# Head attention of a four-layer graph network: eight batches written out, the weighted sums carried over the batch boundary

## The chip, the cores and the metric

The kernel runs on one core of one Trainium2 chip, in one launch. The metric is the device time in microseconds; three runs of a kernel give its median. A profile is one further execution, with its own time beside its span.

## The reference, cut to what matters

Four graph layers act on x of shape (8, 2048, 128) with one 2048 x 2048 adjacency. Layers 0 and 3 are graph attention with one head, layer 2 is a mean over neighbours. The change touches layer 1 alone, attention with 4 heads of 32 features over all nodes:

```
q = (x @ W_q).reshape(Bn, Nn, NUM_HEADS, HEAD_DIM).transpose(0, 2, 1, 3)
k = (x @ W_k)...    # the same shape
v = (x @ W_v)...    # the same shape
scores = jnp.einsum('bhnd,bhmd->bhnm', q, k) / np.sqrt(HEAD_DIM).astype(np.float32)
scores = jnp.where(adj == 0, -jnp.inf, scores)
attn = jax.nn.softmax(scores, axis=-1)
out = jnp.einsum('bhnm,bhmd->bhnd', attn, v)
```

## The kernel before

The kernel is a row of stages, each with a program of its own for TensorE (pe), VectorE (dve), ScalarE (act), GpSimd (pool) and SyncE (sp), tied by semaphores. `head_attention` is the longest. For each batch it takes the four heads as two pairs (u = 0, 1), each pair's 2048 query rows as four chunks of 512, and each chunk against the 2048 keys as T = 16 tiles of 128. So a batch is eight chunks of 16 steps, BODY = 128 steps, and the stage is 8 x 128 = 1024 steps. A step g does this:

- pe: a *slot* (L1175 to L1191), two small matmuls of q and k into `mx_ps`, from which the row maximum of the chunk two further on is found; then the two *scores* matmuls of the step, one for each head, into `sc_ps` (L1231); then `weigh` (L1193 to L1207), the weighted sum of the step LAG = 3 earlier, `w` times `v` into `o_ps`, in float32.
- act: two exponentials from `sc_ps` to `w` (L1314); at the step LAG after a chunk's end, `keep_rows` copies the chunk's sums from `o_ps` to `oe` (L1303).
- pool masks `w` in three steps of four (L1327), dve in the fourth (L1276). dve also takes the maxima of the slot (two reductions, L1263), and once in a chunk joins them (L1270) and writes the row shift `mshift` (L1252).
- sp, once in a chunk, stores the chunk before (`store`: four DMAs) and sends the shift through memory into the extra row of `qs` (`place_shift`: one DMA, a wait for it, two DMAs). At chunk 4 it loads q and k of the next batch for pair 0 (`load`: twelve DMAs) and `v`; at the batch's end the same for pair 1. Each load waits until the scores (or sums) that read the old contents are done.

`w` has PB = 4 buffers, `sc_ps` and `mx_ps` two each, `o_ps` and `oe` two, by the chunk's parity.

All engines run the batches as a hardware loop (`Fori(0, B)`, L1150, L1216, L1287, L1308, L1321) whose body is the 128 steps written out. The counts that they wait for depend on the loop's variable, so they are worked out in registers before the wait. In the loop, pe does `weigh` for steps 0 to 124 in steps 3 to 127 and then the last three in a row (L1238, L1239), and only then branches back; act keeps the last chunk's rows there (L1317). In the last batch the slots of chunks 6 and 7 find maxima for two chunks that do not exist, and sp loads batch 0 once more (`following`).

Of the kernel before, what the change touches and what calls it, by code (L numbers as in the profile page):

```python
# [18 lines left out]
B = 8  # L19
N = 2048  # L20
F = 128
T = N // P
# [3 lines left out]
CH = N // BANK  # L26
# [1012 lines left out]
def head_attention(nc, io, keep):  # L1039
# [11 lines left out]
    BODY = 2 * STEPS  # L1051
    CHUNKS = 2 * CH
    RT = T // CH
    UNITS = RT * CH
    TURN = UNITS // 4
# [4 lines left out]
    with ExitStack() as stack:  # L1060
# [47 lines left out]
        def of_step(jt):  # L1108

            return [k for k, n in enumerate(slots(False)) if (TURN if n < 0 else n) == jt]  # L1110

        def ring(k, chunk_parity):

            return (k + chunk_parity) % MB
# [13 lines left out]
        @block.sync  # L1128
        def _(sp):
            load(sp, 0, 0)  # L1130
            for t in range(T):
                sp.dma_start(mbias[:, t, :], io["mask_bias"][t * P:(t + 1) * P, :]).then_inc(
                    mbias_early if t < 2 * RT else mbias_loaded, 16)
            load_v(sp, 0, 0)
            load(sp, 0, 1)
            load_v(sp, 0, 1)
            place_shift(sp, 0, 0, 0)

            def store(b, c):

                sp.wait_ge(o_kept, 2 * CH * b + c + 1 + 2)
                u, rows = c // CH, slice(c % CH * BANK, (c % CH + 1) * BANK)
                for a in range(2):
                    head = 2 * u + a
                    sp.dma_start(io["heads_t"][bass.ds(b, 1), head * HD:(head + 1) * HD, rows].rearrange("one p n -> p (one n)"),
                                 oe[2 * HD * a:2 * HD * a + HD, c % 2, :]).then_inc(o_stored[c % 2], 16)
                    sp.dma_start(io["sums"][bass.ds(b, 1), head:head + 1, rows].rearrange("one p n -> p (one n)"),
                                 oe[2 * HD * a + HD:2 * HD * a + HD + 1, c % 2, :]).then_inc(o_stored[c % 2], 16)

            with sp.Fori(0, B) as b:  # L1150
                following = (b + 1) % B
                for c in range(CHUNKS):
                    if c == CH:
                        sp.wait_ge(scored, 2 * (BODY * b + STEPS))
                        load(sp, following, 0)
                    if c >= 1:
                        store(b, c - 1)
                    place_shift(sp, CHUNKS * b + c + 1, (c + 1) % CHUNKS // CH, (c + 1) % CH)
                    if c == CH:
                        sp.wait_ge(weighed, BODY * b + STEPS + PB)  # L1160
                        load_v(sp, following, 0)
                sp.wait_ge(scored, 2 * BODY * (b + 1))
                load(sp, following, 1)
                store(b, CHUNKS - 1)
                sp.wait_ge(weighed, BODY * (b + 1) + PB)
                load_v(sp, following, 1)
            for u in range(2):
                sp.wait_ge(qk_loaded[u], LOADS * (B + 1))
                sp.wait_ge(v_loaded[u], 16 * (B + 1))
                sp.wait_ge(o_stored[u], 64 * CH * B)  # L1170
            sp.wait_ge(shift_placed, 32 * (CHUNKS * B + 1))

        @block.tensor
        def _(pe):
            def slot(k, chunk, u, c, first=False):  # L1175

                n, buf = slots(first)[k], ring(k, c % 2)
                if n < 0 and first:
                    return
                if n < 0:  # L1180
                    pe.wait_ge(rows_done, chunk)
                pe.wait_ge(mx_taken, SLOTS * chunk + k + 1)
                if n < 0:
                    mm = nc.tensor.transpose(mx_ps[0:2 * RT, buf, 0, 0:P], mrow[:], keep["ident"][:])
                else:
                    t, kc = RT * c + n // CH, n % CH
                    for a in range(2):
                        hi = slice(a * HD, (a + 1) * HD)
                        mm = nc.tensor.matmul(mx_ps[:, buf, a, :], qs[u][a][hi, t * P:(t + 1) * P], ks[u][a][hi, kc * BANK:(kc + 1) * BANK],  # L1189
                                              start=True, stop=True)  # L1190
                mm.then_inc(mx_scored, 1)  # L1191

            def weigh(g, i):  # L1193

                u, c, jt = g // STEPS, g // T, g % T
                if jt == 0:
                    pe.wait_ge(o_kept, 2 * CH * i + c + 1)
                if g % STEPS == 0:
                    pe.wait_ge(v_loaded[u], 16 * (i + 1))
                if g in mine:  # L1200
                    pe.wait_ge(masked_dve, len(mine) * i + mine.index(g) + 1)
                else:
                    pe.wait_ge(masked_pool, (BODY - len(mine)) * i + g - sum(m < g for m in mine) + 1)
                for a in range(2):
                    mm = nc.tensor.matmul(o_ps[2 * HD * a:2 * HD * a + HD + 1, c % 2, :], v[u][:, jt, a, :], w[:, g % PB, a, :],  # L1205
                                          start=(jt == 0), stop=(jt == T - 1))
                mm.then_inc(weighed, 1)  # L1207

            pe.sem_inc(weighed, PB)
            pe.sem_inc(mx_scored, 1)  # L1210
            pe.wait_ge(qk_loaded[0], LOADS)
            for chunk in range(2):
                for k in range(SLOTS):
                    slot(k, chunk, 0, chunk, chunk == 0)
            pe.wait_ge(units_ready, 4)
            with pe.Fori(0, B) as i:  # L1216
                for g in range(BODY):
                    u, r = g // STEPS, g % STEPS
                    c, jt = r // T, r % T
                    on, tu, tc = target(g // T)  # L1220
                    if jt == 0 and tc == 0:
                        pe.wait_ge(qk_loaded[tu], LOADS * (i + on + 1))
                    mine_now = of_step(jt)
                    slot(mine_now[0], CHUNKS * i + g // T + 2, tu, tc)
                    if jt == 0:
                        pe.wait_ge(shift_placed, 32 * (CHUNKS * i + g // T + 1))
                    for a in range(2):
                        n = 2 * g + a

                        pe.wait_ge(exp_done, 2 * BODY * i + (n + 1 if n else SB))  # L1230
                        nc.tensor.matmul(sc_ps[:, n % SB, :], ks[u][a][:, jt * P:(jt + 1) * P],  # L1231
                                         qs[u][a][:, c * BANK:(c + 1) * BANK], start=True, stop=True).then_inc(scored, 1)

                    if g >= LAG:
                        weigh(g - LAG, i)
                    for k in mine_now[1:]:
                        slot(k, CHUNKS * i + g // T + 2, tu, tc)
                for g in range(BODY - LAG, BODY):  # L1238
                    weigh(g, i)  # L1239

        @block.vector
        def _(dve):
            def slot(k, chunk, c, parity, masks, first=False):

                n, buf = slots(first)[k], ring(k, c % 2)
                if n < 0 and first:
                    return
                due = SLOTS * chunk + k + 1
                if n < 0:
# [4 lines left out]
                    dve.wait_ge(shift_ready, chunk)  # L1254
                    dve.sem_inc(mx_taken, 1)
                else:
                    if not isinstance(due, int):
                        dve.compute_val(due)
                    dve.wait_ge(*masks)
                    dve.wait_ge(mx_scored, due)  # L1260
                    t, kc = RT * c + n // CH, n % CH
# [22 lines left out]
            for chunk in range(2):  # L1284
                for k in range(SLOTS):
                    slot(k, chunk, chunk, chunk, (mbias_early, 16 * 2 * RT), chunk == 0)
            with dve.Fori(0, B) as i:  # L1287
                for g in range(BODY):
                    if g >= 1:
                        mask(g - 1, i)  # L1290
                    for k in of_step(g % T):
                        slot(k, CHUNKS * i + g // T + 2, target(g // T)[2], g // T % 2, (mbias_loaded, 16 * (T - 2 * RT)))
                mask(BODY - 1, i)

        @block.scalar
        def _(act):
# [8 lines left out]

            act.sem_inc(exp_done, SB)
            act.sem_inc(o_kept, 2)
            with act.Fori(0, B) as i:  # L1308
                for g in range(BODY):
                    act.wait_ge(weighed, BODY * i + g + 1)  # L1310
                    for a in range(2):
                        n = 2 * g + a
                        act.wait_ge(scored, 2 * BODY * i + n + 1)
                        nc.scalar.activation(w[:, g % PB, a], sc_ps[:, n % SB], ACT.Exp, scale=SCALE).then_inc(exp_done, 1)  # L1314
                    if g >= T + LAG and (g - LAG) % T == 0:
                        keep_rows((g - LAG) // T - 1, i)
                keep_rows(2 * CH - 1, i)  # L1317

        @block.gpsimd
        def _(pool):  # L1320
            with pool.Fori(0, B) as i:  # L1321
                for g in range(BODY):
                    if g in mine:
                        continue
# [533 lines left out]
```

## Time and profile before

| | |
|---|---|
| median of 3 runs | 3907.07 us (3902.50 to 3911.31) |
| the profiled execution, its own time | 3912.55 us |
| its span, first to last instruction | 3910.80 us |
| busy in the span | PE 3535.3 us (90%), DVE 3162.2 (81%), POOL 1820.8 (47%), ACT 1732.2 (44%) |
| mean granted TensorE clock | 0.939 |
| exponentials of the head attention, first start | 931.3 us |
| its last sums start | 2877.00 us |

The span is 1.75 us shorter than the execution's own time. The stage of the change takes half of the span, from about 930 to about 2880 us. PE, DVE, ACT and POOL are the busy times of matmul, VectorE, ScalarE and GpSimd; PEld is the weight load beside the matmuls; SPq, PEldq are the instructions on an engine's queue that are not counted as busy. In timelines, the bracket is the idle time ahead of a row and what ended it; "issue" means that the profile shows nothing that the engine waited for. Rows that follow each other on an engine are merged in timelines.

### The profile page before, as it was taken

To read this page: it belongs to the slowest core of one execution; us is meant where nothing else is said; L and a number is where in the kernel's file an instruction comes from. 1 tells how busy PE (TensorE), PEld (TensorE's weight loads), DVE (VectorE), ACT (ScalarE), POOL (GpSimd) and SP (SyncE) were. 2 spreads that over 40 slices of the span, in tenths; PEclk is the share of its full clock that TensorE was granted. 3 is DMA by queue.
4 is the path that set the end of the run, shared out by engine and by line. 5 is a ranking of instruction groups with operands and counts; after the bars stand their busy time and mean duration, and the time that the engine had idled before them with its cause. 6 is when DMAs were issued, how large, how long until landed. Compare 5 with 4: busy or idle time off the path is not lost. (4 is left out here: it accounts for less than half of the span.)

```text
span 3910.8 us, 71249 instructions
## 1 busy us (share of the span) xinstructions
PE 3535.3 (90%) x21228; PEld 1849.5 (47%) x21228; DVE 3162.2 (81%) x7145; ACT 1732.2 (44%) x3560; POOL 1820.8 (47%) x854
## 2 busy tenths in 40 slices
PE   5669999666999999999999999999968799789999
PEld 4669999441111111111111111111116599689999
DVE  6768888658999989999898998989967555367777
ACT  7811111552656656566565665656625423311100
POOL 2300000113888878888888887888843101100000
PEclk8779999886999999999999999999977799899999
DMA  6422121462100110001101010100125534221211
GB/s 238 168 100 82 50 87 50 154 232 104 27 19 14 29 27 27 21 12 29 27 27 26 8 27 27 27 23 11 28 90 210 199 144 155 101 91 68 82 65 45
DMA packets 66868, 288.66 MB, mean 74 GB/s; under 512 B 12483, under 2 KB 14917, under 8 KB 47045
## 3 DMA queue, kind: packets, MB, share of 16 engines
q1 hardware_dynamic: 64228, 267.55, 19.5%
q0 software_dynamic: 2304, 16.84, 1.0%
q8 instruction: 185, 3.03, 0.3%
q14 instruction: 151, 1.23, 0.1%
HBM read 174.12 MB, written 110.23 MB: 73 GB/s over the span
## 5 line engine op out<-in xcount | busy, mean ns | idle before, releaser
L1327 POOL TENSOR_TENSOR a_w<-a_w,keep_mask_t 128x1024 f32<-128x1024 f32 x768 | 1635.7, 2155 | 407.2 <-ACT a_w L1314 407.1
L1263 DVE CUSTOM_DVE_ANT_0 a_mx_ps<-a_mx_ps,a_mbias 128x512 f32<-128x512 f32 x2112 | 1389.4, 719 | 142.1 <-PE a_mx_ps L1189 129.6
L1314 ACT ACTIVATE a_w<-a_sc_ps 128x512 f32<-128x512 f32 x2048 | 1111.4, 595 | 812.3 <-PE a_sc_ps L1231 810.9
L1205 PE MATMUL a_o_ps<-a_w,a_v 128*33 128x512 f32 x4096 | 1083.6, 609 | 5.7 <-POOL a_w L1327 5.7
L839 PE MATMUL g_acc<-g_hv,g_w 128*128 128x129 f32 x8192 | 924.5, 276 | 36.4 <-ACT g_hv L797 24.8
L839 PEld LDWEIGHTS g_acc<-g_hv,g_w 128*128 128x128 f32 x8192 | 923.1, 193 | 38.1 <-DVE g_w L776 38.1
L776 DVE SCALAR_TENSOR_TENSOR g_w<-g_row,keep_s,keep_mask_t 128x1024 f32<-128x1024 f32 x512 | 647.2, 1282 | 203.7 <-PE g_acc L839 184.4
L1231 PE MATMUL a_sc_ps<-a_qs,a_ks 97*128 97x512 f16 x2048 | 634.4, 392 | 0.0
L1189 PEld LDWEIGHTS a_mx_ps<-a_ks,a_qs 32*128 32x128 f16 x2112 | 94.8, 91 | 893.9 <-DVE a_mx L1263 469.3
L1189 PE MATMUL a_mx_ps<-a_ks,a_qs 32*128 32x512 f16 x2112 | 411.3, 396 | 77.5 <-DVE a_mx L1263 33.4
L1276 DVE TENSOR_TENSOR a_w<-a_w,keep_mask_t 128x1024 f32<-128x1024 f32 x256 | 460.2, 1798 | 0.7
L1205 PEld LDWEIGHTS a_o_ps<-a_w,a_v 128*33 128x33 f32 x4096 | 151.4, 109 | 449.0 <-issue 287.6
L1263 DVE DVE_READ_ACCUMULATOR2_ANT a_mx<- 128x1 f32 x2112 | 288.8, 137 | 0.0
L1231 PEld LDWEIGHTS a_sc_ps<-a_qs,a_ks 97*128 97x128 f16 x2048 | 125.9, 97 | 241.6 <-issue 201.8
L1757 PE MATMUL p_sum_ps<-p_g,keep_mask_t 128*128 (+1 forms) x2048 | 232.4, 275 | 3.0 <-DMA p_g<-g 3.0
L919 POOL MEMSET p_minus_half<- 128x16 f32 x1 | 0.1, 116 | 493.5 <-POOLq L664 493.5
L1757 PEld LDWEIGHTS p_sum_ps<-p_g,keep_mask_t 128*128 128x128 bf16 x2048 | 201.8, 99 | 27.3 <-DMA p_g<-g 3.1
L101 POOL TENSOR_TENSOR p_rstd<-p_tmp,p_minus_half 128x16 f32<-128x16 f32 x24 | 69.8, 2910 | 290.7 <-DVE p_tmp L88 290.7
L794 ACT COPY g_value<-keep_s 128x16 f32 (+1 forms) x16 | 3.3, 204 | 437.6 <-DMA g_h<-h_nodes 425.8
L803 ACT ACTIVATE g_e<-g_y 128x1024 f32<-128x1024 f32 x16 | 16.9, 1058 | 328.8 <-DVE g_y L741 328.8
L1672 DVE SCALAR_TENSOR_TENSOR p_part<-p_sum_ps,keep_rdeg,p_own 128x128 f32<-128x128 f32 x128 | 44.6, 349 | 121.0 <-PE p_sum_ps L1757 119.9
L1735 ACT ACTIVATE p_hn<-p_x,p_shift,p_rstd 128x128 f32<-128x128 f32 x128 | 50.1, 479 | 115.9 <-DVE p_shift L94 115.9
(178 smaller groups left out, 2278.2 us busy)
## 6 DMA issues: line engine op xcount, KB each, us to landing
p_x<-x SPq DMA_DIRECT2D x24, 1024.0 KB, 8.3
g_h<-h_nodes SPq DMA_DIRECT2D x16, 1032.0 KB, 6.2
p_adj_in<-in_adj SPq DMA_DIRECT2D x16, 1024.0 KB, 7.8
g_row<-u_rows SPq DMA_DIRECT2D x32, 512.0 KB, 7.3
a_v<-v SPq DMA_DIRECT2D x18, 528.0 KB, 3.6
a_ks<-k_hi SPq DMA_DIRECT2D x72, 128.0 KB, 2.8
a_qs<-q_hi SPq DMA_DIRECT2D x72, 128.0 KB, 3.0
v<-p_v SPq DMA_DIRECT2D x8, 1056.0 KB, 6.8
```

Source lines behind the costliest of these rows:

```text
L101: nc.gpsimd.tensor_tensor(rstd, tmp[:, 3, :], minus_half, ALU.pow).then_inc(rooted, 1)
L776: nc.vector.scalar_tensor_tensor(out=w[:, g % PB, :], in0=row[:, k, cols], scalar=keep["s2_08"][:, bass.ds(b, 1), jt], in1=keep["mask_t"][ ...
L839: mm = nc.tensor.matmul(tile(half, it), w[:, g % PB, it * P:(it + 1) * P], hv[:, k, jt, :], start=(jt == 0 and it % 3 == 0), stop=(jt == T ...
L1189: mm = nc.tensor.matmul(mx_ps[:, buf, a, :], qs[u][a][hi, t * P:(t + 1) * P], ks[u][a][hi, kc * BANK:(kc + 1) * BANK], start=True, stop=True)
L1205: mm = nc.tensor.matmul(o_ps[2 * HD * a:2 * HD * a + HD + 1, c % 2, :], v[u][:, jt, a, :], w[:, g % PB, a, :], start=(jt == 0), stop=(jt = ...
L1231: nc.tensor.matmul(sc_ps[:, n % SB, :], ks[u][a][:, jt * P:(jt + 1) * P], qs[u][a][:, c * BANK:(c + 1) * BANK], start=True, stop=True).the ...
L1263: last = nc.vector.tensor_tensor_reduce(out=mx_ps[:, buf, a, :], in0=mx_ps[:, buf, a, :], in1=mbias[:, t, kc * BANK:(kc + 1) * BANK], scal ...
L1276: nc.vector.tensor_tensor(w[:, g % PB], w[:, g % PB], keep["mask_t"][:, jt, c * BANK:(c + 1) * BANK].unsqueeze(1).to_broadcast([P, 2, BANK ...
L1314: nc.scalar.activation(w[:, g % PB, a], sc_ps[:, n % SB], ACT.Exp, scale=SCALE).then_inc(exp_done, 1)
L1327: nc.gpsimd.tensor_tensor(w[:, g % PB], w[:, g % PB], keep["mask_t"][:, jt, c * BANK:(c + 1) * BANK].unsqueeze(1).to_broadcast([P, 2, BANK ...
L1735: last = nc.scalar.activation(hn[:, t, :], x3[:, t, :], ACT.Relu, bias=shift[:, t:t + 1], scale=rstd[:, t:t + 1])
L1757: mm = nc.tensor.matmul(sum_ps[:, it % SLOTS, 0:2 * F], keep["mask_t"][:, jt, it * P:(it + 1) * P], of(g, b)[:, 0, jt, :], start=(jt == 0) ...
```

## The change

All five loops over the batches become Python loops, so that 8 x 128 steps are written out and every count is a constant. pe does the sums of steps 125 to 127 of a batch in steps 0 to 2 of the next batch; act keeps the last chunk's rows after step 3 of the next batch; sp stores them at the next batch's first chunk and loads pair 1's `v` behind that store, ahead of the shift of chunk 1. In the last batch sp loads nothing, the shift for the chunk that does not exist is not placed, and `wanted` leaves out the slots from chunk 64 on, other than the first four of chunk 64 and the transpose of the real last chunk's maxima.

```diff
--- before.py
+++ after.py
@@ -1109,6 +1109,12 @@
 
             return [k for k, n in enumerate(slots(False)) if (TURN if n < 0 else n) == jt]
 
+        def wanted(n, chunk):
+
+
+
+            return chunk < CHUNKS * B or chunk == CHUNKS * B and n in (-1, *range(TURN))
+
         def ring(k, chunk_parity):
 
             return (k + chunk_parity) % MB
@@ -1147,35 +1153,36 @@
                     sp.dma_start(io["sums"][bass.ds(b, 1), head:head + 1, rows].rearrange("one p n -> p (one n)"),
                                  oe[2 * HD * a + HD:2 * HD * a + HD + 1, c % 2, :]).then_inc(o_stored[c % 2], 16)
 
-            with sp.Fori(0, B) as b:
-                following = (b + 1) % B
+            for b in range(B):
+                more = b < B - 1
                 for c in range(CHUNKS):
-                    if c == CH:
+                    if c == CH and more:
                         sp.wait_ge(scored, 2 * (BODY * b + STEPS))
-                        load(sp, following, 0)
+                        load(sp, b + 1, 0)
                     if c >= 1:
                         store(b, c - 1)
-                    place_shift(sp, CHUNKS * b + c + 1, (c + 1) % CHUNKS // CH, (c + 1) % CH)
-                    if c == CH:
+                    elif b > 0:
+                        store(b - 1, CHUNKS - 1)
+                        sp.wait_ge(weighed, BODY * b + PB)
+                        load_v(sp, b, 1)
+                    if more or c < CHUNKS - 1:
+                        place_shift(sp, CHUNKS * b + c + 1, (c + 1) % CHUNKS // CH, (c + 1) % CH)
+                    if c == CH and more:
                         sp.wait_ge(weighed, BODY * b + STEPS + PB)
-                        load_v(sp, following, 0)
-                sp.wait_ge(scored, 2 * BODY * (b + 1))
-                load(sp, following, 1)
-                store(b, CHUNKS - 1)
-                sp.wait_ge(weighed, BODY * (b + 1) + PB)
-                load_v(sp, following, 1)
+                        load_v(sp, b + 1, 0)
+                if more:
+                    sp.wait_ge(scored, 2 * BODY * (b + 1))
+                    load(sp, b + 1, 1)
+            store(B - 1, CHUNKS - 1)
             for u in range(2):
-                sp.wait_ge(qk_loaded[u], LOADS * (B + 1))
-                sp.wait_ge(v_loaded[u], 16 * (B + 1))
                 sp.wait_ge(o_stored[u], 64 * CH * B)
-            sp.wait_ge(shift_placed, 32 * (CHUNKS * B + 1))
 
         @block.tensor
         def _(pe):
             def slot(k, chunk, u, c, first=False):
 
                 n, buf = slots(first)[k], ring(k, c % 2)
-                if n < 0 and first:
+                if n < 0 and first or not wanted(n, chunk):
                     return
                 if n < 0:
                     pe.wait_ge(rows_done, chunk)
@@ -1213,15 +1220,16 @@
                 for k in range(SLOTS):
                     slot(k, chunk, 0, chunk, chunk == 0)
             pe.wait_ge(units_ready, 4)
-            with pe.Fori(0, B) as i:
+            for i in range(B):
                 for g in range(BODY):
                     u, r = g // STEPS, g % STEPS
                     c, jt = r // T, r % T
                     on, tu, tc = target(g // T)
-                    if jt == 0 and tc == 0:
+                    chunk = CHUNKS * i + g // T + 2
+                    if jt == 0 and tc == 0 and chunk < CHUNKS * B:
                         pe.wait_ge(qk_loaded[tu], LOADS * (i + on + 1))
                     mine_now = of_step(jt)
-                    slot(mine_now[0], CHUNKS * i + g // T + 2, tu, tc)
+                    slot(mine_now[0], chunk, tu, tc)
                     if jt == 0:
                         pe.wait_ge(shift_placed, 32 * (CHUNKS * i + g // T + 1))
                     for a in range(2):
@@ -1233,17 +1241,19 @@
 
                     if g >= LAG:
                         weigh(g - LAG, i)
+                    elif i > 0:
+                        weigh(BODY + g - LAG, i - 1)
                     for k in mine_now[1:]:
-                        slot(k, CHUNKS * i + g // T + 2, tu, tc)
-                for g in range(BODY - LAG, BODY):
-                    weigh(g, i)
+                        slot(k, chunk, tu, tc)
+            for g in range(BODY - LAG, BODY):
+                weigh(g, B - 1)
 
         @block.vector
         def _(dve):
             def slot(k, chunk, c, parity, masks, first=False):
 
                 n, buf = slots(first)[k], ring(k, c % 2)
-                if n < 0 and first:
+                if n < 0 and first or not wanted(n, chunk):
                     return
                 due = SLOTS * chunk + k + 1
                 if n < 0:
@@ -1254,8 +1264,6 @@
                     dve.wait_ge(shift_ready, chunk)
                     dve.sem_inc(mx_taken, 1)
                 else:
-                    if not isinstance(due, int):
-                        dve.compute_val(due)
                     dve.wait_ge(*masks)
                     dve.wait_ge(mx_scored, due)
                     t, kc = RT * c + n // CH, n % CH
@@ -1284,7 +1292,7 @@
             for chunk in range(2):
                 for k in range(SLOTS):
                     slot(k, chunk, chunk, chunk, (mbias_early, 16 * 2 * RT), chunk == 0)
-            with dve.Fori(0, B) as i:
+            for i in range(B):
                 for g in range(BODY):
                     if g >= 1:
                         mask(g - 1, i)
@@ -1305,7 +1313,7 @@
 
             act.sem_inc(exp_done, SB)
             act.sem_inc(o_kept, 2)
-            with act.Fori(0, B) as i:
+            for i in range(B):
                 for g in range(BODY):
                     act.wait_ge(weighed, BODY * i + g + 1)
                     for a in range(2):
@@ -1314,11 +1322,13 @@
                         nc.scalar.activation(w[:, g % PB, a], sc_ps[:, n % SB], ACT.Exp, scale=SCALE).then_inc(exp_done, 1)
                     if g >= T + LAG and (g - LAG) % T == 0:
                         keep_rows((g - LAG) // T - 1, i)
-                keep_rows(2 * CH - 1, i)
+                    if g == LAG and i > 0:
+                        keep_rows(2 * CH - 1, i - 1)
+            keep_rows(2 * CH - 1, B - 1)
 
         @block.gpsimd
         def _(pool):
-            with pool.Fori(0, B) as i:
+            for i in range(B):
                 for g in range(BODY):
                     if g in mine:
                         continue
```

## Rows read from the trace of the kernel before

**Rows 1.** Page: busy line of PE, and the granted clock in 40 slices, tenths.
```profile
PE 3535.3 (90%) x21228; PEld 1849.5 (47%) x21228; DVE 3162.2 (81%) x7145; ACT 1732.2 (44%) x3560; POOL 1820.8 (47%) x854
PEclk8779999886999999999999999999977799899999
```

**Rows 2.** Windows inside a batch: busy PE, PEld, DVE, ACT, POOL, clock, DMA share, GB/s.
```profile
2675.00:2822.30 147.30, 147.30 (x647) 28.46 (x645) 141.18 (x351) 91.98 (x171) 127.63 (x61) 1.00 0.08 20
```

**Rows 3.** ScalarE's timeline: `keep_rows`, inside a batch and at batch ends.
```profile
1170.88 1.17 ACT L1303 COPY a_oe<-a_o_ps 33x512 f32<-33x512 f32 x2 [3.61 <-PE a_o_ps L1205]
...
1456.13 1.16 ACT L1303 COPY a_oe<-a_o_ps 33x512 f32<-33x512 f32 x2
...
1632.91 1.16 ACT L1303 COPY a_oe<-a_o_ps 33x512 f32<-33x512 f32 x2
...
1901.78 1.17 ACT L1303 COPY a_oe<-a_o_ps 33x512 f32<-33x512 f32 x2 [3.61 <-PE a_o_ps L1205]
...
2144.58 1.17 ACT L1303 COPY a_oe<-a_o_ps 33x512 f32<-33x512 f32 x2 [3.61 <-PE a_o_ps L1205]
...
2878.10 1.17 ACT L1303 COPY a_oe<-a_o_ps 33x512 f32<-33x512 f32 x2 [3.61 <-PE a_o_ps L1205]
```

**Rows 4.** TensorE's timeline inside a batch: start, length, operation.
```profile
1308.84 0.39 PE L1189 MATMUL a_mx_ps<-a_ks,a_qs 32*128 32x512 f16 x2
1309.16 0.60 PE L1231 MATMUL a_sc_ps<-a_qs,a_ks 97*128 97x512 f16 x2
1309.70 1.05 PE L1205 MATMUL a_o_ps<-a_w,a_v 128*33 128x512 f32 x4
1310.68 0.39 PE L1189 MATMUL a_mx_ps<-a_ks,a_qs 32*128 32x512 f16 x2
```

**Rows 5.** TensorE's timeline over the second batch boundary.
```profile
1409.14 2.77 PE L1205 MATMUL a_o_ps<-a_w,a_v 128*33 128x512 f32 x12
1412.62 1.05 PE L1205 MATMUL a_o_ps<-a_w,a_v 128*33 128x512 f32 x4 [0.71 <-POOL a_w L1327]
1417.76 0.61 PE L1189 MATMUL a_mx_ps<-a_ks,a_qs 32*128 32x512 f16 x2 [4.09 <-issue]
...
1423.78 1.92 PE L1205 MATMUL a_o_ps<-a_w,a_v 128*33 128x512 f32 x4
```

**Rows 6.** TensorE's loop branch: duration ns min/median/max, first and last start.
```profile
L1216 PEldq COMPARE_BRANCH  x8: 79/4144/4905, 1169.9 to 2877.1; - x8
```

**Rows 7.** Window after the second boundary, columns as in rows 2.
```profile
1423.00:1425.00 2.00, 2.00 (x6) 0.30 (x5) 2.00 (x6) 1.13 (x3) 1.88 (x1) 0.50 0.00 0
```

**Rows 8.** SyncE: `load` in mid-batch, first and last of twelve; a `place_shift`.
```profile
1291.58 0.33 SPq L1088 DMA_DIRECT2D a_ks<-k_hi  x1
...
1296.73 0.37 SPq L1091 DMA_DIRECT2D a_qs<-q_lo  x1
...
1426.46 0.28 SPq L1122 DMA_DIRECT2D shifts<-a_mshift  x1
1427.65 0.51 SPq L1125 DMA_DIRECT2D a_qs<-shifts  x2
```

**Rows 9.** Register work ahead of `weigh`, 1310.65 to 1310.85 us.
```profile
L1203 PEldq ALU_OP  x1: 32/32/32, 1310.7 to 1310.7; - x1
```

**Rows 10.** GpSimd's masks, min/median/max ns; three of them in its timeline.
```profile
L1327 POOL TENSOR_TENSOR a_w<-a_w,keep_mask_t x99: 2116/2128/2397, 1175.9 to 1425.3; 128x1024 f32<-128x1024 f32 x99
...
1400.98 6.40 POOL L1327 TENSOR_TENSOR a_w<-a_w,keep_mask_t 128x1024 f32<-128x1024 f32 x3 [0.85 <-ACT a_w L1314]
```

**Rows 11.** SyncE at the stage's end; DMA sizes and us to landing.
```profile
2880.92 0.23 SPq L1147 DMA_DIRECT2D sums<-a_oe  x1
2881.43 0.37 SPq L1095 DMA_DIRECT2D a_v<-v  x1
...
L1169 SPq EVENT_SEMAPHORE  x1: 27/27/27, 2885.0 to 2885.0; - x1
...
x<-g_o SPq DMA_DIRECT2D x16, 512.0 KB, 2.6
```

## The prediction

> **What bounds the kernel now.** I read the page first. PE is busy for 90% of the span, and the granted clock in its 40 slices sits at 9 through the middle, where the head attention is [rows 1]. A digit of 9 can hide a short fall of the clock; the boundaries below show one.
>
> Then the inside of a batch. In a stretch of five whole chunks TensorE is busy all of 147.30 us, at a clock of 1.00; VectorE 141.18, GpSimd 127.63, ScalarE 91.98 [rows 2]. ScalarE copies the sums out once in 16 steps, so its copies are a ruler: from 1456.13 to 1632.91 us there are six chunks in 176.78 us, 29.463 us each, 1.8415 us a step [rows 3]. The 147.30 us are thus 80 steps, and VectorE needs 1.765 us of each, GpSimd 1.595, ScalarE 1.15. TensorE's own timeline gives the step: the slot takes from 1308.84 to 1309.16 (0.32 us), the two scores to 1309.70 (0.54), the weighted sum to 1310.68 (0.98), and then the next slot starts [rows 4]. That is 1.84 us with nothing between, so inside a batch TensorE sets the pace.
>
> Over a boundary it is another picture. The sums of steps 124 to 126 start at 1409.14; those of step 127 wait 0.71 us more for GpSimd's last mask and start at 1412.62; then TensorE has nothing the profile can name for 4.09 us, up to 1417.76, and the first sums of the new batch start at 1423.78, 1.92 us long instead of 1.05 [rows 5]. The idle time is the loop's branch: eight of them, the middle one 4.14 us, the longest 4.9; the shortest, 0.08, is the way out at the end [rows 6]. Behind the pause the granted clock is 0.50, the 1.2 GHz level, while inside a batch it is 1.00, the 2.4 GHz level [rows 7, 2]. So a boundary costs three things: an emptied pipeline, the branch, and some steps at half the clock.
>
> **Part 1, the joined boundaries: 57.3 us.** I price all three together, with the ruler. The last copies of the eight batches run from 1170.88 to 2878.10: 1707.22 us for seven periods, 243.89 each [rows 3]. Eight chunks at 29.463 are 235.70 us. So a boundary costs 8.18 us, seven cost 57.3. The shortest of the seven periods is 2144.58 - 1901.78 = 242.80 [rows 3], which by itself would make 7 x 7.10 = 49.7 us: my lower bound. The eighth boundary is the end of the stage, which still drains, so it gives nothing here.
>
> All of it goes only if steps 0 to 3 of a batch run at 1.84 us like the others. TensorE then does in each of them one slot, two scores, one sum, just what a step in mid-batch does, so its pace is 1.84 again. What is moved has to find its place:
>
> - Sums of chunk 7 use one bank of `o_ps`, chunk 0 the other. The sums of chunk 1, at step 19, need the copy of chunk 7, which ScalarE makes after step 3. It is the same order as at every chunk change inside a batch, and those are inside the 29.463. The copy, 1.16 us [rows 3], is covered by the 0.69 us a step that ScalarE has free.
> - SyncE's queue. After the last scores it issues twelve loads, in mid-batch from 1291.58 to 1297.10, 5.5 us [rows 8]. The store of chunk 7 waits for the copy after step 3: about 4 x 1.84 + 1.2 = 8.6 us after the last scores. The store's four DMAs and the one of `v` are issued 0.5 us apart [rows 11], 2.5 us: 11.1. Then the shift of chunk 1: the second DMA follows the first by 1.19 us and takes 0.51 to issue [rows 8]; for its landing I allow the 2.6 us of a DMA of 512 KB [rows 11], as its own is not shown. That is 15.4 us, and TensorE asks for the shift at step 16, 29.5 us after. 14 us to spare. VectorE, whose next write of `mshift` needs the first of these DMAs landed, comes later still.
> - The pair-1 `v` is wanted at step 67, the pair-1 q and k at step 32: far off.
> - That twelve loads run under full work is nothing new. The pair-0 load does it at mid-batch, from 1291.58, and the steps of 1308.84 and after are as all others [rows 8, 4].
>
> The registers: each step of TensorE loses about four operations of 32 ns, and VectorE and ScalarE lose some. I price them at nothing. The one ahead of `weigh` ran at 1310.7, but the sums it belongs to started at 1311.5, one step after 1309.70 [rows 9, 4]: the queue is fed 0.8 us ahead, so the array sets the pace and not the sequencer. If that cover were not there, the four would cost 4 x 32 ns, 0.13 us of a step: it is the third rival.
>
> **Part 2, the slots left out: 6.1 us.** 12 slots of chunk 64 and 16 of chunk 65 go, all in the last 28 steps of the last batch. TensorE's step falls to 1.84 - 0.32 = 1.52 us [rows 4]. But GpSimd masks three steps in four, at 2.13 us each, and three in a row take 6.40 [rows 10]; with a little between them I take 6.45 us for four steps, 1.61 a step. So GpSimd becomes the bound of these steps, and not TensorE. It has about 1 us of slack in a group of four now, which is used up first: one group of 7.37 - 6.72 = 0.64 us gain, then six of 7.366 - 6.45 = 0.92, together 6.1 us. Bounds: nothing, if the masks come late for another reason, and 28 x 0.32 = 9.0 us, if TensorE stays the bound. VectorE loses 1.3 us of work a step there, which shortens nothing, as it is not waited for.
>
> **Part 3, the end of the stage: 1.7 us.** SyncE issues the last store at 2880.92, then a load of `v` that nobody uses at 2881.43, and is past its wait for that at 2885.0, 3.6 us later; only then can the stage end [rows 11]. Without the load it waits for the store alone. Its landing isn't shown; with the 2.6 us of the 512 KB store it is 2883.5 [rows 11], which gives 1.5, and the twelve needless loads ahead of it no longer hold up the store's issue, some 0.2. Bounds 0 and 2.3. The Trainium skill, "DMA: Bandwidth & Descriptors", on what the fixed cost is made of, puts about 2.0 us on any transfer; with that, an estimate, the store would land at 2882.9 and part 3 would be 2.3. No run here shows it yet.
>
> **The sum.** 57.3 + 6.1 + 1.7 = 65.1 us. Against the profiled execution's own time (its span plus 1.75 us) it is 3912.55 - 65.1 = 3847.4. The median of the runs shown is 5.5 us below that execution. If this difference lies elsewhere, the new median is 3907.07 - 65.1 = 3842.0; if it lies in the boundaries, whose branches differ by a microsecond or more from one to the next, it is 3847. I take 3844.
>
> **The rivals.**
>
> *Straight-line code starves (slower, 3%).* Eight times the instructions are each fetched once, in one stream. If a block of them came late now and then, TensorE would stand as it does at the branch, 4.1 us a time [rows 6]. The gain is gone at 65 / 4.1 = 16 such stops, two in a batch; one in every chunk would be 64 x 4.1 - 65 = 197 us slower, 4104. Against it: the body of 128 steps is already straight-line code, and its chunks are 29.463 us long with no stop in six of them [rows 3], also while loads fill the DMA queues. That two stops a batch appear only because a branch is gone has nothing for it.
>
> *The clock does not hold (slower or same, 2%).* With no pause for 1880 us TensorE might be granted less. Each 1% would cost about 0.015 us a step (the array's share of the 1.84), 15 us in all; 4.3% would eat the gain. Against it: 1.00 in a stretch of 147 us [rows 2].
>
> *The step itself gets shorter (faster than forecast, 5%).* The slot, scores and sum take 0.32, 0.54 and 0.98 us, though 512, 2 x 512 and 4 x 512 columns at 2.4 GHz are 0.21, 0.43 and 0.85: 0.35 us of a step are something else. If it is the register work or the waits it feeds, constants remove part of it, down to VectorE's 1.765 us [rows 2]. That is 0.077 x 1024 = 78 us on top, 3766. Against it: at the boundary the sums of three steps, with the same registers between them, take 2.77 us together, 0.92 each with the tail of the last counted in [rows 5], so the registers cost nothing there; the 0.35 us come at the change from one kind of matmul to another. The Trainium skill, "TensorE: Matmul & The Clock Gate", on the array's layout, says that TensorE's queue can pull weight loads ahead of matmuls in flight; it would bring this case about if registers are what keeps it from doing so here. The trace doesn't show that they are.
>
> *The boundary closes only in part (6%).* Some wait stays: the masks of steps 125 to 127, or SyncE's chain. With the 0.71 us wait for GpSimd and the refill of about 2 us at each of seven, 19 us are kept, and it is 3863. Against it: the masks in mid-batch are in time for sums three steps later, and SyncE has 14 us.
>
> **How the numbers follow.** The forecast has 84%. A difference of 0.2%, 7.8 us, is about what a measurement of this kernel can tell. Faster: forecast, shorter step and partial closing, 95%; same 2%; slower 3%. Within the forecast the low end is 57.3 + 9.0 + 2.3 off 3907.07, 3838.5, and with a difference between runs of some 4 us 3834; the high end is 49.7 off, 3857. The partial closing lies just beyond; 3858 leaves out about 18%.
>
> **What the profile after should show.** Copies of `keep_rows` 29.46 us apart through all 63 gaps but the last two, which are shorter; the last batch's first 100 steps unchanged. No gap of TensorE over 1 us between 940 and 2800 us, clock 1.00 all through, mean clock over the span up from 0.939. In the last 28 steps a step of about 1.61 us with the weighted sums waiting for GpSimd. The copy that ends the stage 63.4 us sooner after the first one. The prediction is wrong if stops with "issue" ahead of them appear inside the stream, if the step leaves 1.84 us, or if the boundary steps show a wait for the shift or for `o_ps`.

## The result and the profile after

The changed kernel takes 3848.88 us (median of 4 runs, 3847.42 to 3852.25); the kernel before, in 4 runs, 3907.97 us (3902.50 to 3911.31). The ratio is 0.9851, with a 95% interval of 0.9834 to 0.9868: 59 us less. The forecast was 3844, with a range of 3833 to 3858. Between the profiled executions the difference is a little larger, 3912.55 to 3848.57, 64.0 us.

The page of the changed kernel: TensorE's busy line, and the granted clock. They answer to the page's busy figures of before and to [rows 1].

```profile
PE 3507.7 (91%) x21171; PEld 1850.8 (48%) x21171; DVE 3132.1 (81%) x7030; ACT 1731.4 (45%) x3560; POOL 1816.2 (47%) x854
...
PEclk8779999886999999999999999999977799899999
```

Two stretches of the changed kernel in the windows view (columns as in [rows 2]): the head attention up to the last chunks, over seven boundaries, and its last 42 us.

```profile
950.00:2770.00 1820.00, 1818.91 (x7962) 354.77 (x7960) 1744.72 (x4316) 1136.07 (x2101) 1568.93 (x741) 1.00 0.08 22
2777.00:2819.00 42.00, 35.88 (x135) 7.08 (x134) 14.20 (x6) 23.83 (x44) 41.98 (x18) 0.96 0.01 4
```

In the first TensorE rests for 1.1 us out of 1820, and the clock is 1.00 throughout. In the second GpSimd is the engine that never rests, 41.98 of 42.00 us.

TensorE's timeline over the first boundary of the changed kernel, which answers to [rows 4, 5]. The scores of step 127 are those of 1164.78; the rows from 1166.30 on belong to the next batch.

```profile
1164.78 0.60 PE L1239 MATMUL a_sc_ps<-a_qs,a_ks 97*128 97x512 f16 x2
1165.31 1.05 PE L1212 MATMUL a_o_ps<-a_w,a_v 128*33 128x512 f32 x4
1166.30 0.39 PE L1196 MATMUL a_mx_ps<-a_ks,a_qs 32*128 32x512 f16 x2
1166.62 0.61 PE L1239 MATMUL a_sc_ps<-a_qs,a_ks 97*128 97x512 f16 x2
1167.15 1.05 PE L1212 MATMUL a_o_ps<-a_w,a_v 128*33 128x512 f32 x4
1168.14 0.39 PE L1196 MATMUL a_mx_ps<-a_ks,a_qs 32*128 32x512 f16 x2
```

The boundary is not to be seen any more: slot to slot is 1.84 us, as in mid-batch, and the sums of steps 124 and 125, at 1165.31 and 1167.15, stand where a step's sums always stand, those of 125 behind the first slot and scores of the next batch.

SyncE's timeline behind the same boundary: first load, first store, `v`, and the two halves of the shift's way through memory.

```profile
1165.41 0.32 SPq L1088 DMA_DIRECT2D a_ks<-k_hi  x1
...
1174.79 0.33 SPq L1151 DMA_DIRECT2D heads_t<-a_oe  x1
...
1176.48 0.36 SPq L1095 DMA_DIRECT2D a_v<-v  x1
1176.88 0.33 SPq L1128 DMA_DIRECT2D shifts<-a_mshift  x1
1180.07 0.51 SPq L1131 DMA_DIRECT2D a_qs<-shifts  x2
```

The shift is issued 15.2 us after the first load. TensorE wants it at step 16, 29.5 us after step 0.

ScalarE's last copies of sums in the changed kernel, the ruler of [rows 3].

```profile
2765.70 1.16 ACT L1311 COPY a_oe<-a_o_ps 33x512 f32<-33x512 f32 x2
...
2792.89 1.16 ACT L1311 COPY a_oe<-a_o_ps 33x512 f32<-33x512 f32 x2
...
2820.24 1.17 ACT L1311 COPY a_oe<-a_o_ps 33x512 f32<-33x512 f32 x2 [5.88 <-PE a_o_ps L1212]
```

Up to 2765.70 the gaps between copies are 29.46 us, at the boundaries too, but for five of 29.75 (and one of 29.35 between two of them). The last two gaps are 27.19 and 27.35 us. In the kernel before they were 29.46 and 25.82, as the last copy of a batch comes 3.6 us early, by two steps, when its last three sums follow each other directly. So the last two chunks take 54.54 us instead of 55.28: that is all that the left-out slots brought.

The masks of the last 42 us, GpSimd's and VectorE's (min/median/max ns), and three rows of these engines' timelines:

```profile
L1337 POOL TENSOR_TENSOR a_w<-a_w,keep_mask_t x18: 2119/2126/3111, 2775.5 to 2816.9; 128x1024 f32<-128x1024 f32 x18
L1284 DVE TENSOR_TENSOR a_w<-a_w,keep_mask_t x6: 1996/2626/3195, 2775.5 to 2810.8; 128x1024 f32<-128x1024 f32 x6
...
2770.98 48.00 POOL L1337 TENSOR_TENSOR a_w<-a_w,keep_mask_t 128x1024 f32<-128x1024 f32 x20 [0.62 <-ACT a_w L1322]
...
2804.50 3.17 DVE L1284 TENSOR_TENSOR a_w<-a_w,keep_mask_t 128x1024 f32<-128x1024 f32 x1 [6.15 <-ACT a_w L1322]
2810.76 2.07 DVE L1284 TENSOR_TENSOR a_w<-a_w,keep_mask_t 128x1024 f32<-128x1024 f32 x1 [3.09 <-ACT a_w L1322]
```

Four of GpSimd's masks there, one by one:

```profile
2804.47 2.12 POOL L1337 TENSOR_TENSOR a_w<-a_w,keep_mask_t 128x1024 f32<-128x1024 f32 x1
2806.56 3.10 POOL L1337 TENSOR_TENSOR a_w<-a_w,keep_mask_t 128x1024 f32<-128x1024 f32 x1
2809.63 2.12 POOL L1337 TENSOR_TENSOR a_w<-a_w,keep_mask_t 128x1024 f32<-128x1024 f32 x1
2811.71 3.11 POOL L1337 TENSOR_TENSOR a_w<-a_w,keep_mask_t 128x1024 f32<-128x1024 f32 x1
```

Twenty masks of GpSimd take 48.00 us, 2.40 each, against the 2.13 of [rows 10]: 5.4 us more than twenty times 2.13. And VectorE's go up to 3.2 us. The two engines' masks take turns: VectorE's, started at 2804.50, ends at 2807.67, 1.08 us after GpSimd's of 2804.47, and GpSimd's next ends at 2809.66, 1.99 us after VectorE's. Four steps, three masks of GpSimd, take 7.24 us (2804.47 to 2811.71).

### The profile page after: what moved, and what is told of

The parts are those of the page before. It is cut to its first block and busy times, and to the rows that moved or that the text cites. A ratio compares the mean times of both kernels' runs of the same rounds, so it can differ in the third digit from the quotient of the medians.

```text
span 3847.0 us, 61721 instructions
## 1 busy us (share of the span) xinstructions
PE 3507.7 (91%) x21171; PEld 1850.8 (48%) x21171; DVE 3132.1 (81%) x7030; ACT 1731.4 (45%) x3560; POOL 1816.2 (47%) x854
## 5 line engine op out<-in xcount | busy, mean ns | idle before, releaser
L1271 DVE CUSTOM_DVE_ANT_0 a_mx_ps<-a_mx_ps,a_mbias 128x512 f32<-128x512 f32 x2056 | 1352.4, 719 | 83.2 <-PE a_mx_ps L1196 70.6
L1239 PE MATMUL a_sc_ps<-a_qs,a_ks 97*128 97x512 f16 x2048 | 621.5, 385 | 0.3
L1196 PE MATMUL a_mx_ps<-a_ks,a_qs 32*128 32x512 f16 x2056 | 395.6, 392 | 52.4 <-DVE a_mx L1271 33.3
L1271 DVE DVE_READ_ACCUMULATOR2_ANT a_mx<- 128x1 f32 x2056 | 281.1, 137 | 0.0
```

The lines of the kernel that those rows point to most:

```text
L1271: last = nc.vector.tensor_tensor_reduce(out=mx_ps[:, buf, a, :], in0=mx_ps[:, buf, a, :], in1=mbias[:, t, kc * BANK:(kc + 1) * BANK], scal ...
```

## The experiments

The stretch ahead of the head attention is the same in all kernels, yet the first copy of sums comes at 962.3 to 970.0 us from profile to profile. So I read the parts off the copies inside the stage, and the whole off the medians. The ratios are to the kernel before, run beside each experiment; "changed" is the changed kernel's first profile. The diffs are cut to the lines that matter.

**e1: the sums carried, the loops kept.** TensorE and ScalarE have batch 0 written out and loop over the other seven; slots and loads at the end are those of the kernel before.

```diff
+            def batch(i):
                 ...
                     if g >= LAG:
                         weigh(g - LAG, i)
+                    elif not isinstance(i, int):
+                        weigh(BODY + g - LAG, i - 1)
...
+            batch(0)
+            with pe.Fori(1, B) as i:
+                batch(i)
+            for g in range(BODY - LAG, BODY):
+                weigh(g, B - 1)
```

> The kernel before with its loops, but the sums of steps 125 to 127 and the copy of the last chunk carried into the next batch (batch 0 is written out for TensorE and ScalarE, the loop runs over the other seven). This is the carrying alone. Theory A: the branch and the half clock behind it make up most of the 8.18 us of a boundary, and the drain little; six boundaries still have a branch (the first is straight), so the copies at the boundaries lie 29.46 + 5 to 7 us apart and the whole is 10 to 25 us below the kernel before, about 3890. Rival B: the drain was the main cost, the branch then hides behind other engines' work: 40 us or more below, 3865.

Measured: 3878.35 us (ratio 0.9925, 0.9908 to 0.9941). The two gaps at a boundary are 31.75 to 33.02 and 29.78 us, on average 3.2 us over two plain ones. Seven of these are 22.6 us. My expectation counted six branches, and the branch view below has six besides the way out, the first at 1405.1; but there are seven stops. At the first boundary TensorE has no branch. It waits for VectorE's maxima, and VectorE has stood still behind the branch of its own loop:

```profile
1172.85 0.70 DVE L1269 CUSTOM_DVE_ANT_0 a_mx_ps<-a_mx_ps,a_mbias 128x512 f32<-128x512 f32 x1 [3.40 <-issue]
...
1174.32 0.39 PE L1189 MATMUL a_mx_ps<-a_ks,a_qs 32*128 32x512 f16 x2 [2.28 <-DVE a_mx L1269]
```

VectorE, GpSimd and SyncE still loop in e1, so what is left there is not TensorE's branch alone. TensorE's timeline at the second boundary, and its branches:

```profile
1408.67 0.54 PE L1189 MATMUL a_mx_ps<-a_ks,a_qs 32*128 32x512 f16 x2 [1.94 <-issue]
1409.14 1.03 PE L1231 MATMUL a_sc_ps<-a_qs,a_ks 97*128 97x512 f16 x2
1410.11 1.92 PE L1205 MATMUL a_o_ps<-a_w,a_v 128*33 128x512 f32 x4
...
L1242 PEldq COMPARE_BRANCH  x7: 83/3418/3755, 1405.1 to 2839.3; - x7
```

The branch takes 3.4 us, but only 1.94 of it are idle time for the array: it starts at 1405.1, while the array still has the scores of 1405.14 and the sums of 1405.68 ahead of it. One step then runs at half the clock: its sums take 1.92 us. Over the seven boundaries TensorE's stops are 1.8 to 2.3 us, against 3.1 to 4.1 behind the drained queue of the kernel before. In the kernel before the branch stood behind a wait for the last mask, so nothing covered it. Neither of my two figures was right: the carrying alone brings 8.18 - 3.2 = 5.0 us a boundary, more than theory A gave it and less than rival B. The whole is 29.7 us below the kernel before.

**e2: written out, but drained at each batch's end.** The changed kernel with the old order of the last sums.

```diff
-                    elif i > 0:
-                        weigh(BODY + g - LAG, i - 1)
...
-            for g in range(BODY - LAG, BODY):
-                weigh(g, B - 1)
+                for g in range(BODY - LAG, BODY):
+                    weigh(g, i)
...
-                    if g == LAG and i > 0:
-                        keep_rows(2 * CH - 1, i - 1)
-            keep_rows(2 * CH - 1, B - 1)
+                keep_rows(2 * CH - 1, i)
```

> The changed kernel with the sums of steps 125 to 127 done at the batch's end again, ahead of the next batch's first slot, and the copy with them: writing out alone. Theory A: no branch, no fall of the clock, only the emptied pipeline: TensorE waits 0.7 us for GpSimd and refills, 2 to 3 us a boundary, seven of them 14 to 21 us above the changed kernel, 3866 or so; granted clock 1.00 over the boundary. Rival B: the drain was the main cost: 35 us or more above it.

Measured: 3877.29 us (ratio 0.9920, 0.9904 to 0.9937). The gap over a boundary is 36.55 to 38.17 us, on average 37.14; with the 25.82 before it that is 4.03 us over two plain gaps, 28.2 us in all. TensorE's timeline over the second boundary, and a window behind it:

```profile
1411.35 1.05 PE L1212 MATMUL a_o_ps<-a_w,a_v 128*33 128x512 f32 x4 [0.77 <-POOL a_w L1333]
...
1414.29 0.88 PE L1239 MATMUL a_sc_ps<-a_qs,a_ks 97*128 97x512 f16 x2 [0.71 <-ACT a_w L1320]
...
1417.59 1.92 PE L1212 MATMUL a_o_ps<-a_w,a_v 128*33 128x512 f32 x4
...
1417.00:1421.00 4.00, 4.00 (x13) 0.73 (x12) 3.77 (x10) 1.81 (x5) 3.92 (x2) 0.63 0.26 105
```

There is no pause of 4 us here, and still the clock falls, to a mean of 0.63 in this window: sums of 1.92 us, as at 0.50 in [rows 5, 7], are sums at the 1.2 GHz level. Theory A left that out and gave 2 to 3 us; it was 4.03. Rival B's 35 us were not reached either. What went before the fall is TensorE waiting 0.77 us for a mask and then doing steps without sums, with waits for ScalarE. So each half of the change alone is worth 4.2 (e2) or 5.0 us (e1) of a boundary's 8.18, and what is left in the one, 4.03, and in the other, 3.2, makes 7.2: the two costs nearly add, and 0.9 us arise only where both are there.

**e3: the unused slots put back,** and with them the shift for the chunk that does not exist.

```diff
-            return chunk < CHUNKS * B or chunk == CHUNKS * B and n in (-1, *range(TURN))
+            return True
```

> The changed kernel with the unused slots of the last batch and the shift placed for nothing put back. My prediction's term: 6.1 us slower than the changed kernel. What its trace says instead: the copies of the last two chunks gained 2.3 us and lost 1.5 again, so 0.5 to 1 us slower and no more, 3849.5; the last step's sums then wait for GpSimd 1.6 us as in the kernel before.

Measured: 3846.59 us (3844.17 to 3849.85; ratio 0.9845, 0.9828 to 0.9861), not to be told from the changed kernel. Its last two gaps are 29.46 and 25.82 us, 55.28 together: 0.74 us more than with the slots left out. My term of 6.1 us is out; what the trace said holds.

**e4: the needless loads put back.**

```diff
-                if more:
-                    sp.wait_ge(scored, 2 * BODY * (b + 1))
-                    load(sp, b + 1, 1)
+                sp.wait_ge(scored, 2 * BODY * (b + 1))
+                load(sp, (b + 1) % B, 1)
             store(B - 1, CHUNKS - 1)
+            sp.wait_ge(weighed, BODY * B + PB)
+            load_v(sp, 0, 1)
+            sp.wait_ge(qk_loaded[1], LOADS * (B + 1))
+            sp.wait_ge(v_loaded[1], 16 * (B + 1))
```

> The changed kernel with the thirteen needless loads at the end of the last batch put back, and the waits for them. From the last copy of the head attention to the reciprocal of the next stage it was 15.6 us in the kernel before and 12.6 us in the changed one. If the loads are the cause, this kernel has 15.6 again and is 3.0 us slower than the changed one; my prediction's term was 1.7. If the 3.0 come from elsewhere (the order of the queue, the shorter program), it stays at 12.6.

Measured: 3852.52 us (ratio 0.9855, 0.9838 to 0.9871). From the last copy to the reciprocal it takes 14.76 us, against 12.64 in the changed kernel and 15.61 before. So the loads are worth 2.1 us. The other 0.85 come with constants on SyncE: in the changed kernel a store follows the one before it by 0.36 us where it was 0.5. From the last copy to the issue of `v` it is 2.57 us in e4 and 3.33 in the kernel before, which is 0.76 of the 0.85; e1, with registers on SyncE, has 15.55 in all.

The same profile has a surprise in the last chunks: 30.20 and 25.76 us, longer than with all slots. A window of that stretch:

```profile
2784.00:2790.00 6.00, 6.00 (x14) 0.72 (x16) 0.00 (x0) 1.82 (x4) 6.00 (x3) 0.50 0.00 0
```

With less to do and waits for masks (1.47 us for the one ahead of it), TensorE falls to half the clock, in the midst of the tail. Nothing that e4 puts back comes before this point, and the changed kernel waits there just as long, yet its clock stays at 1.00:

```profile
2785.89 1.05 PE L1212 MATMUL a_o_ps<-a_w,a_v 128*33 128x512 f32 x4 [1.48 <-POOL a_w L1337]
...
2784.00:2790.00 6.00, 4.53 (x19) 0.83 (x17) 0.00 (x1) 3.26 (x6) 6.00 (x4) 1.00 0.00 0
```

So the fall belongs to this execution and not to the loads; it made the two chunks 1.4 us longer. Whether it could come at all without the slots left out is not shown. In the changed kernel's last 42 us the mean clock was 0.96, with the fall at the very end.

**e5: VectorE's masks of the last 28 steps left out.** The weights of these seven steps stay unmasked, so part of the output is that of another sum. The sums wait for the exponentials instead. The diff shows VectorE's part.

```diff
             def mask(g, i):
-                if g in mine:
+                if g in mine and not (i == B - 1 and g >= BODY - 28):
```

> The changed kernel without VectorE's seven masks in the last 28 steps of the last batch (these steps' weights stay unmasked; the sums wait for the exponentials alone). In the changed kernel VectorE's masks there take 3.17 us, and one in three of GpSimd's takes 3.10 instead of 2.12. Theory A, the two engines' masks shut each other out: GpSimd's masks are all 2.12 us, four steps take 6.4, and the last copy comes 6 to 7 us sooner after the copy at step 99 than in the changed kernel. Rival B, GpSimd is slow there for a reason of its own (its masks back to back): its masks keep a 3.1 in each group and the time stays.

Measured: 3842.54 us (ratio 0.9831, 0.9815 to 0.9848). The last two gaps are 24.92 and 23.33 us, 48.25 together, 6.3 less than in the changed kernel. GpSimd's masks there:

```profile
L1339 POOL TENSOR_TENSOR a_w<-a_w,keep_mask_t x22: 2130/2150/2157, 2765.9 to 2810.4; 128x1024 f32<-128x1024 f32 x22
```

Not one above 2.16 us, though they are back to back here as well. So rival B is out: it is VectorE's masks that made GpSimd's long. Against e3, with slots and masks, the two chunks gain 7.0 us: what the prediction had put at 6.1.

**e6 and e7: who masks in the last 28 steps.** e6 gives VectorE every second mask there, e7 all of them. The counts that TensorE waits for follow.

```diff
+    MINE = [g for g in range(BODY) if g % 4 == 1]
+    TAIL = BODY - 28
+    MINE_LAST = [g for g in MINE if g < TAIL] + [g for g in range(TAIL, BODY) if g % 2 == 1]   # e7: if True
+
+    def mine_of(i):
+        return MINE_LAST if i == B - 1 else MINE
...
-                if g in mine:
+                if g in mine_of(i):
```

> The changed kernel with every second mask of the last 28 steps on VectorE instead of every fourth. Theory A: the masks of both engines run one after the other, 2 x 2.12 + 2 x 1.0 = 6.3 us for four steps against 7.34 now, so 1.57 a step, 7 us faster than the changed kernel in all, and VectorE's masks are seen to last over 2 us each for the wait in them. Rival B: they run side by side, TensorE is the bound at 1.52 a step and VectorE's masks are near 1.2: 9 us faster.

> The changed kernel with all masks of the last 28 steps on VectorE, which has nothing else to do there. Theory A: nobody shuts anybody out, a mask takes 1.2 us as the shortest of VectorE's in mid-batch, TensorE is the bound at 1.52 a step: 28 x 0.32 = 9 us sooner than the kernel with slots, and the last steps' sums wait less, 1 to 2 us more, so 9 to 11 us faster than the changed kernel, 3839. If VectorE's mask is slow for itself (1.9 us as its middle value in mid-batch), the steps stay at 1.9 and nothing is gained.

Measured: e6 3838.16 us (ratio 0.9819, 0.9803 to 0.9836), last two gaps 24.86 and 22.08; e7 3840.24 us (0.9828, 0.9811 to 0.9844), 24.86 and 21.53. The masks of both in the tail, first e6:

```profile
L1344 POOL TENSOR_TENSOR a_w<-a_w,keep_mask_t x15: 2127/2388/2632, 2765.2 to 2807.1; 128x1024 f32<-128x1024 f32 x15
...
L1291 DVE TENSOR_TENSOR a_w<-a_w,keep_mask_t x14: 1872/2103/2297, 2768.2 to 2808.5; 128x1024 f32<-128x1024 f32 x14
```

and e7:

```profile
L1291 DVE TENSOR_TENSOR a_w<-a_w,keep_mask_t x28: 1214/1226/1348, 2767.8 to 2809.3; 128x1024 f32<-128x1024 f32 x28
```

Alone, a mask of VectorE is 1.23 us long; beside GpSimd's it is 2.10, with the wait in it. In e6 the last two chunks come 7.6 us sooner than in the changed kernel, nearer to theory A (7) than to rival B (9), and the masks do take turns; and in e7 they come 8.2 us sooner, just short of the 9 to 11 expected. In e7 VectorE does alone, in 1.23 us of a step, what the two engines together held up before.

**e8 and e9: the changed kernel and e7 once more, side by side, five executions each.**

> The changed kernel itself, on one chip with the next one, in five rounds: 3849 us. By the copies in its profile the last two chunks take 54.5 us.

> The changed kernel with all masks of the last 28 steps on VectorE, again, beside the changed kernel on the same chip. Its last two chunks took 46.4 us against 54.5, so it should be 8.1 us faster, 3841. If single runs differ by more in the stages before, the 8 us are only seen between the copies.

Measured: the changed kernel 3846.50 us (3845.26 to 3848.59; ratio 0.9842, 0.9829 to 0.9855), e7's code 3837.05 us (3835.81 to 3842.16; 0.9823, 0.9810 to 0.9836). The difference is 9.5 us between medians and 8.0 between the copies (54.43 against 46.40). Version e7 is faster than both kernels.

| kernel | median, us | extra at a boundary, us | last two chunks, us | last copy to reciprocal, us |
|---|---|---|---|---|
| before | 3907.97 | 8.18 | 55.28 | 15.61 |
| changed | 3848.88 | 0 | 54.54 | 12.64 |
| e1 loops, carried | 3878.35 | 3.2 | 55.29 | 15.55 |
| e2 written out, drained | 3877.29 | 4.03 | 54.42 | 12.61 |
| e3 slots back | 3846.59 | 0 | 55.28 | 13.12 |
| e4 loads back | 3852.52 | 0 | 55.96 | 14.76 |
| e5 no VectorE masks in the tail | 3842.54 | 0 | 48.25 | 12.53 |
| e6 every second mask | 3838.16 | 0 | 46.94 | 12.67 |
| e7 all masks on VectorE | 3840.24 | 0 | 46.39 | 12.30 |
| e8 changed, again | 3846.50 | 0 | 54.43 | 12.64 |
| e9 e7, again | 3837.05 | 0 | 46.40 | 12.37 |

## Why the prediction was right, point by point

**What bounds the kernel.** TensorE in mid-batch, at 1.8415 us a step: a chunk of 29.46 us stood in all eleven profiles, with registers and without.

**Part 1, 57.3 us.** Measured between the first copy and the last: 1909.82 before, 1853.19 after, 56.63 us less, of which 0.74 belong to part 2. So 55.9. The missing 1.4 are five chunks of 29.75 instead of 29.46. In four of them VectorE's reductions start 0.3 us late at the chunk's turn, after 1.45 us of rest instead of 1.10, and TensorE waits 0.23 us for it:

```profile
1028.55 0.70 DVE L1271 CUSTOM_DVE_ANT_0 a_mx_ps<-a_mx_ps,a_mbias 128x512 f32<-128x512 f32 x1 [1.45 <-PE a_mx_ps L1196]
...
1030.02 0.39 PE L1196 MATMUL a_mx_ps<-a_ks,a_qs 32*128 32x512 f16 x2 [0.23 <-DVE a_mx L1271]
```

They are there in every written-out version at the same places, every second batch, and in none of the looped ones inside a batch. If anything here is a trace of the rival in which straight-line code starves, it is this, at a price of 1.4 us in all; the stops of 4 us did not come. What makes VectorE late there I have not tried.

**The moved steps cost nothing.** Right, each by its place. SyncE's chain was forecast to issue the store 8.6 us after the last scores; it came 9.4 us after the first load, and the second half of the shift at 14.7 us. The forecast of 15.4 us had that half's landing in it, and 1.19 us between the two halves; behind `v` it was 3.19 us, so the issue alone was done at 15.2. The slack was thus somewhat less than 14 us, by a landing that no view shows, and it was enough: TensorE did not wait.

**The registers.** Priced at nothing, and nothing it was for TensorE: e1 with registers and the changed kernel without have the same 29.46. With that the rival of a shorter step is out. I had missed that SyncE issues faster with constants, 0.36 us from store to store instead of 0.5.

**Part 2, 6.1 us: the step that failed.** "GpSimd becomes the bound of these steps" was right. The size was not: I took 6.45 us for its three masks, from a stretch in which it has a microsecond of rest in every four steps. (The 6.72 us of that sum's first group I had taken from no row.) VectorE's one mask comes between GpSimd's, and each of the two lasts longer for it by what the other holds; the microsecond of rest takes that up. Without rest it falls on the path: four steps take 7.24 us, 1.81 a step and not 1.61, against 7.37 with slots; that is 5.4 us over the twenty masks, and 0.74 us is left of the gain. So the signs given for the tail failed as well: TensorE rests for 1.48 us at 2784.4, before 2800, and a last copy 56.6 us sooner after the first and not 63.4. e5 shows the cause, e7 the cure. The Trainium skill, "SBUF — State Buffer", "SBUF: two separate sides", says it in a rule that I should have weighed: VectorE and GpSimd share one pair of SBUF ports, and a VectorE operation with two SBUF inputs locks out a GpSimd operation that reads SBUF for its whole length, and the other way round. The traces agree: 1.23 us alone and 2.10 beside GpSimd in e6, GpSimd's 3.11 against 2.13, and the turns of 1.08 and 1.99 us read off above.

**Part 3, 1.7 us.** 2.1 us by e4 for the loads, within the bounds. With the faster issue the end of the stage gained 3.0, which is outside them. The landing of the last store was mis-sized: the prediction took 2.6 us, and the Trainium skill's figure, which its page "DMA: Bandwidth & Descriptors" gives in a section on transfers issued by GpSimd, would be 2.0. In the changed kernel SyncE is past its wait for the store 1.3 us after issuing it:

```profile
2822.48 0.27 SPq L1153 DMA_DIRECT2D sums<-a_oe  x1
...
L1178 SPq EVENT_SEMAPHORE  x1: 17/17/17, 2823.8 to 2823.8; - x1
```

**The sum.** 65.1 forecast, 64.0 between the two profiled executions: 56.6 + 3.0 inside and behind the stage, 1.2 ahead of its first copy, and 3.2 in later stages, in which nothing was changed, so that 60 us are the change's and the rest is how two executions differ. With the medians it is 59.1. The forecast of 3844 is 4.9 us low. By its terms, part 2 was 5.4 us too high, part 1 1.4 too high and part 3 1.3 too low, which makes 59.6 in place of 65.1. That part 3 and the 2 us allowed for the difference between executions offset some of part 2 is luck.

**The rivals.** The clock was 1.00 through the boundaries (first section), so that rival is out. The boundary closed in full: slot to slot is 1.84 us across it, and no mask or shift is waited for.

## What to carry to other kernels

When a long loop over a pipelined body is costed, take the period of a fixed event inside the body as a ruler and read the boundary's whole cost as period minus body: drain, branches and the steps at half the clock come in one figure. A drain ahead of a loop's branch also takes away the queued work that would hide half of the branch. And before an engine's time is taken as the next bound, ask what its present rest absorbs: here it was the turn of the other engine's mask, and the engine that had come free could take the whole job.

## What the runs showed of the hardware

- A taken branch of TensorE's queue took 3.3 to 4.9 us; at the boundary shown, with work queued ahead of it, the array stood idle for 1.94 us only (e1). VectorE stood 3.40 us behind the branch of its own loop (e1).
- The granted clock fell without any long pause: after waits of 0.77 and 0.71 us and steps without their float32 sums (e2, a mean of 0.63 over 4 us), and to 0.50 in the last chunks behind a wait of 1.47 us for a mask (e4). Behind a wait of 1.48 us at the same place the changed kernel kept 1.00.
- A mask of 128 x 1024 float32 by bfloat16 took VectorE 1.23 us alone and 2.10 beside GpSimd's; GpSimd's took 2.15 alone, and up to 3.11 beside VectorE's.
- Eight batches written out, a stream of 1024 steps, ran with 1.1 us of rest for TensorE in 1820 us; no stop for instructions could be seen there, other than perhaps the late starts of VectorE, four waits of 0.23 us for TensorE.
